# A two-layer decoder on one core: the two norms around the last feed-forward move from VectorE to ScalarE, its first products and its transposes move in TensorE's order, and the output leaves tile by tile

## The chip, the cores and the metric

The kernel runs on one core of a Trainium2 chip. A core has five engines, each with an instruction queue of its own: TensorE (PE, matrix products into PSUM), VectorE (DVE), ScalarE (ACT), GpSimd (POOL) and SyncE (SP, which issues most transfers here). They meet only at semaphores. The metric is the device time in microseconds (us) of one launch.

## The reference

Two decoder layers on x (2 x 512 x 512, 1024 token rows). Each layer is self-attention, cross-attention and a feed-forward, and a layer norm without weights follows each addition:

```python
x = _layernorm(x + _L1_attn_ref(x, ...), axis=-1)
x = _layernorm(x + _L1_xattn_ref(x, ctx_1024, mask, ...), axis=-1)
x = _layernorm(x + _L1_ffn_ref(x, w_gate, w_up, w_down, up_idx, down_idx), axis=-1)
```

The last feed-forward quantises each row of its input to fp8 with the row's own scale, multiplies by the quantised gate and up weights (1408 columns each), takes `silu(g) * u`, quantises that row in the same way and multiplies by the down weights:

```python
qx = _fp8(xr / scale_x)                 # scale_x: largest magnitude of the row / 448
y = qx * scale_x @ (qw * w_scale).T * scale
t = jax.nn.silu(g) * u                  # then quantised and multiplied by w_down
```

`_layernorm` is `(x - m) / sqrt(v + 1e-5)` over the 512 columns of a row.

## The kernel before

The 1024 rows are eight tiles of 128 rows (`NT = 8`), kept in `xf`. Six stages run one after the other, `self0, cross0, ffn0, self1, cross1, ffn1`, and every engine has its own hand-written program for all of them, so the order on an engine is the order of the code. Only the end of `cross1` and the whole of `ffn1` matter here.

**The output projection of `cross1`** (PE, `project`) adds 16 heads into one PSUM bank per tile (bank t for tile t), three bfloat16 matmuls of 128x512 per head and tile. Heads 0 to 7 are done first for all tiles. Then, in before.py, heads 8 to 11 of tiles 0 to 3 go together, and a loop over t finishes each tile: 12 matmuls (4 heads) for tiles 0 to 3, 24 matmuls (8 heads) for tiles 4 to 7. The last matmul of a tile adds one to `y_mm`.

**What follows a tile** in `cross1`: DVE adds the residual and takes mean and variance (`residual`, lines 1028 to 1030, `ln_var`); POOL makes the inverse deviation in two instructions (`inv_std`, lines 612 and 613, `ln_rstd`); DVE normalises (`normalise`, line 1036, `ln_x`); DVE takes the row's largest magnitude and three small scale values (`scales`, lines 994 to 997, `x_amax`); ACT writes two scaled copies (`scaled_x`, lines 734 and 735, `x_scaled`); DVE rounds to fp8 steps in three instructions (`round_x`, lines 1001, 1008, 1011, `qx_ok`); PE transposes the result (`turn_qx`, line 1289, `qx_mm`) and ACT copies it from PSUM (`turned_x`, line 740, `qx_T`). `turn_qx` of tile t < 4 writes bank t, of a later tile bank 6 or 7. DVE runs a loop over k: `residual(k)`, `normalise(k - 1)`, `scales` of k - 1, `round_x(k - 2)`. In PE's loop `turn_qx` of tile t - 4 stands behind the projection of tile t (t = 4 to 7).

**The last feed-forward** (`ffn1`): PE's `product(part, t)` (line 1343) makes gate (part 0, banks 0 to 2) and up (part 1, banks 3 to 5) of a tile, twelve matmuls each. DVE scales them out of PSUM (`gate`, line 1077, and `up`, line 1083), ACT applies silu (line 792), DVE multiplies (`rows`, line 1089) and takes the row's scale values, ACT scales (`scaled_rows`, lines 799 and 800), DVE rounds (`round_t`, lines 1001, 1098, 1102), PE transposes (line 1355), ACT copies (`turned_rows`), PE multiplies by the down weights (line 1374), and DVE adds the residual and takes the statistics (`residual`, lines 1022, 1026, 1029, 1030), POOL the inverse deviation, DVE the norm (line 1036). The loop on DVE per tile:

```python
rows(t)
if t + 1 < NT:
    gate(t + 1)
    up(t + 1)
round_t(t)
if t:
    residual(t - 1)
if t > 1:
    normalise(t - 2)
```

At the end SP waits for all eight norms and stores the whole output with one transfer (line 524).

Of the kernel before, what the change touches and what calls it, by code (L numbers as in the profile page):

```python
# [124 lines left out]
def build(nc, a, out, kept):  # L125
    ctx = ExitStack()
    with ctx:
# [18 lines left out]
        mv = sb("mv", [P, NT, 2], F32)  # L146
        rstd = sb("rstd", [P, NT], F32)
        half_neg = sb("half_neg", [P, QT], F32)
# [228 lines left out]
        def _(sp):  # L377
# [23 lines left out]
            for li, L in enumerate(stages):  # L401
# [111 lines left out]
                if L.masked:  # L513
# [8 lines left out]
                    sp.dma_start(mem[names.index("ffn1")]["sB"][:, :], kept["s"].partition_broadcast(P)).then_inc(s_in, 16)  # L522
            sp.wait_ge(ln_x, NT * len(stages))
            sp.dma_start(out.rearrange("b (p e) d -> p b e d", e=4), xf[:, :, :]).then_inc(out_ok, 16)
            sp.wait_ge(out_ok, 16)


        @block.gpsimd
        def _(pool):
# [75 lines left out]
            for li, L in enumerate(stages):  # L605
                c, m = ledger[li], mem[li]

                def inv_std(k):

                    t = tiles(names[li])[k][0]  # L610
                    pool.wait_ge(ln_var, c["ln"] + k + 1)
                    own(nc.gpsimd.tensor_scalar(rstd[:, t:t + 1], mv[:, t, 1:2], EPS, None, ALU.add))
                    nc.gpsimd.tensor_tensor(rstd[:, t:t + 1], rstd[:, t:t + 1], half_neg[:, 0:1], ALU.pow).then_inc(ln_rstd, 1)

# [107 lines left out]
        def _(act):  # L722
            def x_part(li, n, t, bank):

                act.wait_ge(x_mm, n + 1)
                nc.scalar.activation(xT[0][:, :, token_cols(li, t)], ps[:, bank, :].rearrange("p (c n) -> p c n", c=XC), ACT.Copy).then_inc(x_hi, 1)

            def scaled_x(m, t):

                n = X_COL + t  # L730
                act.wait_ge(x_amax, t + 1)
                if t >= 2:
                    act.wait_ge(qx_ok, t - 1)
                nc.scalar.activation(m["xM"][:, t % 2, :], xf[:, t, :], ACT.Copy, scale=q_up[:, n:n + 1])
                nc.scalar.activation(m["xrow"][:, t % 2, :], xf[:, t, :], ACT.Copy, scale=q_inv[:, n:n + 1]).then_inc(x_scaled, 1)
# [18 lines left out]
            for li, L in enumerate(stages):  # L754
# [34 lines left out]
                if names[li] == "ffn1":  # L789
# [18 lines left out]
                    nc.scalar.preload_act_table_set("silu_and_others")  # L808
                    for t in range(4, 6):
                        turned_x(m, t)  # L810
                    gate(0)
                    for t in range(6, NT):
                        turned_x(m, t)
                    for t in range(NT):
                        scaled_rows(t)
                        if t + 1 < NT:
                            gate(t + 1)
                        turned_rows(t)
                    continue

# [102 lines left out]
                if stages[li + 1] is None and names[li + 1] == "ffn1":  # L923
                    for t in range(NT):
                        scaled_x(mem[li + 1], t)
                        if t >= 4:
                            turned_x(mem[li + 1], t - 4)
                else:
                    for t in range(NT):
                        x_part(li + 1, NT * (li + 1) + t, t, t)  # L930
                        if L.rms and t == 1:
                            f = mem[li + 1]
                            act.wait_ge(q_ok, 15)
                            act.wait_ge(o_mm, c["u"] + UNITS)
                            act.wait_ge(q_kept[0], kept_count(15))
                            act.wait_ge(gu_in[0], 16)
                            nc.scalar.activation(f["gu"][0][:, 0, :, :], f["raw_gu"][0], ACT.Copy).then_inc(gu_hi, 1)
# [3 lines left out]
        def _(dve):  # L941
# [49 lines left out]
            def scales(n, src):  # L991
# [4 lines left out]
                own(nc.vector.reciprocal(q_inv[:, col], q_scale[:, col]))  # L996
                return nc.vector.tensor_scalar(q_up[:, col], q_inv[:, col], 2.0 ** 20, None, ALU.mult)

            def steps(M):
# [13 lines left out]
            for li, L in enumerate(stages):  # L1013
# [58 lines left out]
                if names[li] == "ffn1":  # L1072
# [21 lines left out]
                    def round_t(t):  # L1094
# [7 lines left out]
                        nc.vector.scalar_tensor_tensor(out=q, in0=M, scalar=HALF_UP, in1=y, op0=ALU.max, op1=ALU.subtract, reverse1=True).then_inc(qt_ok, 1)  # L1102

                    dve.wait_ge(s_in, 16)
                    gate(0)
                    up(0)
                    for t in range(NT):
                        rows(t)
# [4 lines left out]
                        if t:  # L1113
                            residual(t - 1)
                        if t > 1:
                            normalise(t - 2)
                    residual(NT - 1)
                    normalise(NT - 2)
                    normalise(NT - 1)
                    continue  # L1120
# [125 lines left out]

                last_attention = names[li + 1] == "ffn1"
                for k in range(NT + 3):
                    if k < NT:
                        residual(k)  # L1250
                    if 0 <= k - 1 < NT:
                        normalise(k - 1)
                        if last_attention:
                            dve.wait_ge(ln_x, c["ln"] + k)
                            scales(X_COL + k - 1, xf[:, k - 1, :]).then_inc(x_amax, 1)
                    if 0 <= k - 2 < NT and last_attention:
                        round_x(mem[li + 1], k - 2)
                    if 0 <= k - 3 < NT and not last_attention:
                        x_part(li + 1, NT * (li + 1) + k - 3, k - 3, k - 3)
# [9 lines left out]
        def _(pe):  # L1269
# [11 lines left out]
            def turn_qx(done, m, t):  # L1281
# [6 lines left out]
                for ch in range(XC):  # L1288
                    last = nc.tensor.transpose(ps[:, bank, :].bitcast(BF16)[:, ch * P:ch * P + P], m["xQ"][:, t % 2, ch * P:ch * P + P], idb[:, :])
                last.then_inc(qx_mm, 1)  # L1290

            pe.wait_ge(const_ok, 4)
# [3 lines left out]
            for li, L in enumerate(stages):  # L1296
# [37 lines left out]
                if names[li] == "ffn1":  # L1334
                    def product(part, t):

                        pe.wait_ge(qx_T, max(t + 1, 3 + part))
                        pe.wait_ge(ln_var, c["ln"] - 2)
                        if t:
                            pe.wait_ge(u_ok if part else g_ok, t)  # L1340
                        for n, (lo, hi) in enumerate(CH):
# [15 lines left out]

                    pe.wait_ge(wt_in, 16 * (2 * XC + IT))
                    product(0, 0)
                    product(1, 0)  # L1360
                    turn_qx(c["ln"], m, 4)
                    turn_qx(c["ln"], m, 5)
# [105 lines left out]
                for h in range(8):  # L1468
                    for t in (4, 5):
                        project(t, h, h == 0, False)  # L1470
                for h in range(8, 12):
                    pe.wait_ge(w_split, c["split"] + H + h + 1)
                    for t in range(4):
                        project(t, h, False, False)
                pe.wait_ge(w_split, c["split"] + 2 * H)
                turns = {4: (0, 1), 5: (2, 3), 6: (4,), 7: (5,), 8: (6,), 9: (7,)}
                for t in range(NT + 2):
                    if t < NT:
                        for h in range(12 if t < 4 else 8, H):
                            last = project(t, h, False, h == H - 1)  # L1480
                        last.then_inc(y_mm, 1)
                    if names[li + 1] == "ffn1":
                        if 4 <= t < NT:
                            pe.wait_ge(idb_ok, 1)
                            turn_qx(c["ln"] + t - 3, mem[li + 1], t - 4)
                    else:
# [63 lines left out]
```

## Time and profile before

| | us |
|---|---|
| median of three runs | 2621.8 (2616.11 to 2622.53) |
| the profiled execution, its time | 2614.38 |
| the profiled execution, its span | 2612.6 |
| PE busy | 2438.2 (93%) |
| DVE busy | 1848.3 (71%) |
| ACT busy | 1588.8 (61%) |
| POOL busy | 711.8 (27%) |

The busy shares are means over six unlike stages. The change touches only what runs after about 2425 us, some 190 us, so the table by stretches of time and the timelines of the engines in that part are what to read, not the shares. A time in a row is counted from the start of the span. The profiled execution took 7.4 us less than the median of the three runs.

### The profile page before, as it was taken

How to read it: one execution, taken by the hardware profiler on the slowest of the kernel's cores; microseconds unless marked ns; L12 is line 12 of the kernel's file. 1: busy time of each engine (PE TensorE's matmuls, PEld its weight loads, DVE VectorE, ACT ScalarE, POOL GpSimd, SP SyncE). 2: the span in 40 equal slices, each digit the busy share in tenths (PEclk: the TensorE clock that was granted, in tenths of full speed). 3: DMA queues.
4: the chain of work that ended last, by engine and by line, in shares of the span. 5: the costliest groups of instructions: out<-in, count | busy, mean ns of one | idle time of the engine just before them, and what ended most of it. 6: DMA issues, size and time to landing. Idle time of an engine off the chain costs nothing. (4 is left out here: it accounts for less than half of the span.)

```text
span 2612.6 us, 57672 instructions
## 1 busy us (share of the span) xinstructions
PE 2438.2 (93%) x21584; PEld 1567.4 (60%) x21584; DVE 1848.3 (71%) x3371; ACT 1588.8 (61%) x2718; POOL 711.8 (27%) x671
## 2 busy tenths in 40 slices
PE   7999998989999999999988999999899999999864
PEld 4555555546666666666465666665566666665432
DVE  4777777657777777776665666667578888884597
ACT  5777675158887777886244566553277777773242
POOL 5666665601111111012332222226100000013111
PEclk9999999999999999999988999999999999999987
DMA  2433335325666666667341444445188777777200
GB/s 93 90 76 87 79 82 127 103 55 108 114 118 110 113 109 117 115 108 154 113 169 26 94 93 96 95 93 139 30 146 149 145 147 144 146 149 153 69 1 32
DMA packets 769429, 273.83 MB, mean 105 GB/s; under 512 B 737905, under 2 KB 740721, under 8 KB 767601
## 3 DMA queue, kind: packets, MB, share of 16 engines
q1 hardware_dynamic: 767504, 265.82, 49.0%
q0 software_dynamic: 1760, 5.77, 0.8%
q8 instruction: 110, 1.80, 0.3%
q14 instruction: 55, 0.44, 0.1%
HBM read 84.55 MB, written 6.44 MB: 35 GB/s over the span
## 5 line engine op out<-in xcount | busy, mean ns | idle before, releaser
L881 ACT ACTIVATE phl<-p,ri 128x1024 bf16<-128x1024 f32 (+4 forms) x512 | 437.4, 854 | 414.0 <-DVE ri L1196 386.1
L1206 DVE SCALAR_TENSOR_TENSOR phl<-p,ri,phl 128x1024 bf16<-128x1024 f32 (+4 forms) x512 | 514.1, 1004 | 103.3 <-issue 75.3
L892 ACT ACTIVATE p<-p,nb 128x1024 f32<-128x1024 f32 (+4 forms) x512 | 435.9, 851 | 53.9 <-DVE nb L1189 39.6
L1273 PE MATMUL ps<-wo_lo,v_hi 128*128 128x128 bf16 x2496 | 440.0, 220 | 0.0
L1272 PE MATMUL ps<-wo_hi,v_hi 128*128 128x128 bf16 x2240 | 396.5, 220 | 23.0 <-DMA wo_hi<-phl 15.7
L1274 PE MATMUL ps<-wo_hi,v_lo 128*128 128x128 bf16 x2240 | 396.2, 220 | 0.0
L1272 PE MATMUL ps<-k_hi,q_hi 128*128 128x512 bf16 (+3 forms) x768 | 272.5, 355 | 20.9 <-DVE nb L1187 18.7
L1273 PE MATMUL ps<-k_lo,q_hi 128*128 128x512 bf16 (+3 forms) x768 | 271.9, 354 | 0.0
L1274 PE MATMUL ps<-k_hi,q_lo 128*128 128x512 bf16 (+3 forms) x768 | 271.7, 354 | 0.0
L1273 PEld LDWEIGHTS ps<-wo_lo,v_hi 128*128 128x128 bf16 x2496 | 245.1, 98 | 33.4 <-issue 0.5
L1272 PEld LDWEIGHTS ps<-wo_hi,v_hi 128*128 128x128 bf16 x2240 | 219.5, 98 | 68.0 <-DMA wo_hi<-phl 27.9
L551 POOL TENSOR_SCALAR wkv_hi<-raw_kv 128x1024 bf16<-128x1024 f32 (+1 forms) x56 | 49.2, 878 | 658.9 <-PE ps L1274 509.5
L1274 PEld LDWEIGHTS ps<-wo_hi,v_lo 128*128 128x128 bf16 x2240 | 219.7, 98 | 0.0
L1272 PE MATMUL ps<-xT_hi,wq_hi 128*128 128x512 bf16 x512 | 195.1, 381 | 4.5 <-DVE xT_lo L958 3.5
L1191 DVE CUSTOM_DVE_ANT_0 p<-ps,rk,nq 128x1024 f32<-128x1024 f32 x128 | 163.1, 1274 | 51.3 <-PE ps L1274 51.0
L1273 PE MATMUL ps<-xT_lo,wq_hi 128*128 128x512 bf16 x512 | 195.1, 381 | 0.0
L1274 PE MATMUL ps<-xT_hi,wq_lo 128*128 128x512 bf16 x512 | 195.1, 381 | 0.0
L1272 PE MATMUL ps<-wo_hi,oT_hi 128*128 128x512 bf16 x512 | 194.4, 380 | 0.6 <-DVE nb L1187 0.6
L1273 PE MATMUL ps<-wo_lo,oT_hi 128*128 128x512 bf16 x512 | 194.2, 379 | 0.0
L1274 PE MATMUL ps<-wo_hi,oT_lo 128*128 128x512 bf16 x512 | 194.1, 379 | 0.0
L651 POOL TENSOR_TENSOR nq<-nq,half_neg 128x4 f32<-128x4 f32 x32 | 32.3, 1010 | 549.6 <-DVE nq L1140 549.6
L1189 DVE CUSTOM_DVE_ANT_0 p<-ps,mb 128x1024 f32<-128x1024 f32 x128 | 155.8, 1217 | 36.5 <-PE ps L1274 34.2
(200 smaller groups left out, 6126.5 us busy)
## 6 DMA issues: line engine op xcount, KB each, us to landing
raw_kv<-in_wkvself SPq DMA_DIRECT2D x32, 512.0 KB, 4.0
raw_q<-in_wqself SPq DMA_DIRECT2D x32, 256.0 KB, 2.6
raw_q<-in_woself SPq DMA_DIRECT2D x32, 256.0 KB, 2.8
raw_q<-in_wqcross SPq DMA_DIRECT2D x32, 256.0 KB, 3.0
raw_q<-in_wocross SPq DMA_DIRECT2D x32, 256.0 KB, 3.0
wo_hi<-phl SPq DMA_TRANSPOSE x384, 3.2
wo_lo<-phl SPq DMA_TRANSPOSE x384, 3.1
raw_kv<-in_wkvcross SPq DMA_DIRECT2D x24, 256.0 KB, 3.2
```

The costliest lines, as they stand in the source:

```text
L551: nc.gpsimd.tensor_scalar(hi, src, 1.0, 1.0, ALU.mult, ALU.mult).then_inc(w_hi, 1)
L651: nc.gpsimd.tensor_tensor(r, r, half_neg[:, 0:QT], ALU.pow).then_inc(q_norm, 1)
L881: nc.scalar.activation(m["ph"](qt, w), m["p"][:, qt % 2, 0:w], ACT.Copy, scale=ri[:, qt % 2:qt % 2 + 1]).then_inc(p_norm, 1)
L892: nc.scalar.activation(prob, prob, ACT.Exp, scale=1.0 if L.rms else -1.0, bias=nb[:, qt % 2:qt % 2 + 1], accum_out=rs[:, qt % 2:qt % 2 + 1 ...
L1189: ins = nc.vector.tensor_tensor_reduce(in1=m["mb"][:, L.batch(n), :], scale=-ISQ, op0=ALU.add, **kw)
L1191: ins = nc.vector.tensor_tensor_reduce(in1=m["rk"][:, n % 2, :], scale=m["nq"][:, n % 2, qt:qt + 1], op0=ALU.mult, **kw)
L1206: nc.vector.scalar_tensor_tensor(out=m["pl"](qt, w), in0=m["p"][:, qt % 2, 0:w], scalar=ri[:, qt % 2:qt % 2 + 1], in1=m["ph"](qt, w), op0= ...
L1272: nc.tensor.matmul(o, l(0), r(0), start=first, stop=False)
L1273: nc.tensor.matmul(o, l(0), r(1), start=False, stop=False)
L1274: return nc.tensor.matmul(o, l(1), r(0), start=False, stop=last)
```

## The change

- **Norms on ScalarE.** In `cross1` and `ffn1` (both stand beside `"ffn1"` in the list of stages) POOL's `inv_std` gets a third instruction, `shift = -mean * rstd`, and ACT normalises with `Identity(x * rstd + shift)`. DVE's `normalise` is gone there. In ACT's program the norm of tile t stands ahead of `scaled_x(t - 1)` in `cross1`, and in `ffn1` the norm of tile t - 1 behind `turned_rows(t)`.
- **Projections tile by tile.** In `cross1` (`L.masked`) heads 8 to 15 of tiles 0 to 3 are done tile by tile as well, so each tile is one run of 24 matmuls.
- **Transposes.** `turn_qx` of tile t - 2 stands behind the projection of tile t (t = 2 to 5), where it was tile t - 4 (t = 4 to 7).
- **First products.** Gate and up of tile 0 move into the projection loop, behind the projections of tiles 6 and 7.
- **DVE's order.** In `cross1` the loop ends with `residual(7)`, `scales` of 6, `round_x(5)`; the rest (`scales` of 7, `round_x(6)`, `round_x(7)`) stands around the first `gate` and `up`.
- **Output.** Eight stores of one tile each, every one behind its tile's norm.

```diff
@@ SP
-            sp.wait_ge(ln_x, NT * len(stages))
-            sp.dma_start(out.rearrange("b (p e) d -> p b e d", e=4), xf[:, :, :]).then_inc(out_ok, 16)
-            sp.wait_ge(out_ok, 16)
+            for t in range(NT):
+                sp.wait_ge(ln_x, NT * (len(stages) - 1) + t + 1)
+                sp.dma_start(out.rearrange("b (p e) d -> p b e d", e=4)[:, t // 4, t % 4, :], xf[:, t, :]).then_inc(out_ok, 16)
+            sp.wait_ge(out_ok, 16 * NT)
@@ POOL, inv_std
+                    own(root)
+                    nc.gpsimd.tensor_scalar(shift[:, t:t + 1], mv[:, t, 0:1], rstd[:, t:t + 1], -1.0, ALU.mult, ALU.mult).then_inc(ln_rstd, 1)
@@ ACT
+            def normalise(li, t):
+
+                act.wait_ge(ln_rstd, ledger[li]["ln"] + t + 1)
+                nc.scalar.activation(xf[:, t, :], xf[:, t, :], ACT.Identity, scale=rstd[:, t:t + 1], bias=shift[:, t:t + 1]).then_inc(ln_x, 1)
...
                     for t in range(NT):
-                        scaled_x(mem[li + 1], t)
-                        if t >= 4:
-                            turned_x(mem[li + 1], t - 4)
+                        normalise(li, t)
+                        if t:
+                            scaled_x(mem[li + 1], t - 1)
+                        if 3 <= t < 7:
+                            turned_x(mem[li + 1], t - 3)
...
-                    for t in range(4, 6):
-                        turned_x(m, t)
+                    turned_x(m, 4)
+                    scaled_x(m, NT - 1)
                     gate(0)
-                    for t in range(6, NT):
+                    for t in range(5, NT):
                         turned_x(m, t)
                     for t in range(NT):
                         scaled_rows(t)
                         if t + 1 < NT:
                             gate(t + 1)
                         turned_rows(t)
+                        if t:
+                            normalise(li, t - 1)
+                    normalise(li, NT - 1)
@@ DVE, ffn1
+                    scaled(NT - 1)
                     dve.wait_ge(s_in, 16)
                     gate(0)
+                    round_x(m, NT - 2)
                     up(0)
+                    round_x(m, NT - 1)
...
                         if t:
                             residual(t - 1)
-                        if t > 1:
-                            normalise(t - 2)
                     residual(NT - 1)
-                    normalise(NT - 2)
-                    normalise(NT - 1)
@@ DVE, end of cross1
+                if names[li + 1] == "ffn1":
+                    for k in range(NT):
+                        residual(k)
+                        if k >= 1:
+                            scaled(k - 1)
+                        if k >= 2:
+                            round_x(mem[li + 1], k - 2)
+                    continue
@@ PE, end of cross1
-                for h in range(8, 12):
+                ahead = 0 if L.masked else 4
+                for h in range(8, 8 + ahead):
...
                     if names[li + 1] == "ffn1":
-                        if 4 <= t < NT:
+                        if 2 <= t < 6:
                             pe.wait_ge(idb_ok, 1)
-                            turn_qx(c["ln"] + t - 3, mem[li + 1], t - 4)
+                            turn_qx(c["ln"] + t - 1, mem[li + 1], t - 2)
+                        if t == 6:
+                            first_product(mem[li + 1], 0)
+                        if t == 7:
+                            pe.wait_ge(ln_var, c["ln"] + 6)
+                            first_product(mem[li + 1], 1)
```

**DVE, one round of its loop at the end of `cross1`.** `xf<-ps,xf` is the residual, `xf<-xf,mv,rstd` the norm, `q_max<-xf` the start of the scales, `xQ<-xM,xrow` the end of the rounding. Before:

```order
L1028 TENSOR_TENSOR xf<-ps,xf 128x512 [waits y_mm]
L1029 BN_STATS stat<-xf 128x6 [waits dve_seq]
L1030 BN_AGGR mv<-stat 128x2 [waits dve_seq]
L1036 TENSOR_SCALAR xf<-xf,mv,rstd 128x512 [waits ln_var,ln_rstd]
L994 TENSOR_REDUCE q_max<-xf 128x1 [waits ln_x]
L995 TENSOR_SCALAR q_scale<-q_max 128x1 [waits dve_seq]
L996 RECIPROCAL q_inv<-q_scale 128x1 [waits dve_seq]
L997 TENSOR_SCALAR q_up<-q_inv 128x1 [waits dve_seq]
L1001 TENSOR_SCALAR xM<-xM 128x512 [waits x_scaled]
L1008 SCALAR_TENSOR_TENSOR xrow<-xM,xrow 128x512 [waits dve_seq]
L1011 SCALAR_TENSOR_TENSOR xQ<-xM,xrow 128x512 [waits dve_seq]
```

Now:

```order
L1049 TENSOR_TENSOR xf<-ps,xf 128x512 [waits y_mm]
L1050 BN_STATS stat<-xf 128x6 [waits dve_seq]
L1051 BN_AGGR mv<-stat 128x2 [waits dve_seq]
L1010 TENSOR_REDUCE q_max<-xf 128x1 [waits ln_x]
L1011 TENSOR_SCALAR q_scale<-q_max 128x1 [waits dve_seq]
L1012 RECIPROCAL q_inv<-q_scale 128x1 [waits dve_seq]
L1013 TENSOR_SCALAR q_up<-q_inv 128x1 [waits dve_seq]
L1022 TENSOR_SCALAR xM<-xM 128x512 [waits x_scaled]
L1029 SCALAR_TENSOR_TENSOR xrow<-xM,xrow 128x512 [waits dve_seq]
L1032 SCALAR_TENSOR_TENSOR xQ<-xM,xrow 128x512 [waits dve_seq]
```

The norm is gone and the rest keeps its order: the rounding of tile k - 2 still stands behind the residual of tile k.

**PE, from the last wait for split weights to the first transpose of `xQ`** (`wo` by `oT` is the projection). Before; 119 further projection matmuls stand at the first "...", which end with tile 4:

```order
L1272 MATMUL ps<-wo_hi,oT_hi 128x512 [waits w_split]
...
L1273 MATMUL ps<-wo_lo,oT_hi 128x512
L1274 MATMUL ps<-wo_hi,oT_lo 128x512
L1289 MATMUL ps<-idb,xQ 128x128 [waits ln_var,qx_ok,idb_ok]
L1289 MATMUL ps<-idb,xQ 128x128 x3
```

Now; the run from that row to the transposes is 72 matmuls and ends with tile 2:

```order
L1294 MATMUL ps<-wo_hi,oT_hi 128x512 [waits w_split]
...
L1295 MATMUL ps<-wo_lo,oT_hi 128x512
L1296 MATMUL ps<-wo_hi,oT_lo 128x512
L1311 MATMUL ps<-idb,xQ 128x128 [waits ln_var,qx_ok,idb_ok]
L1311 MATMUL ps<-idb,xQ 128x128 x3
```

The first transposes, which wait for `qx_ok` of tile 0, moved from behind tile 4 to behind tile 2.

**PE, the first products of `ffn1`** (`qxT` is the transposed input). Before, behind the last projection and a transpose:

```order
L1289 MATMUL ps<-idb,xQ 128x128 x3
L1343 MATMUL ps<-xT_hi,qxT 128x512 [waits ln_var,qx_T,wt_in]
...
L1343 MATMUL ps<-xT_lo,qxT 128x384 x2
L1343 MATMUL ps<-cT_hi,qxT 128x512 [waits ln_var,qx_T]
```

Now, gate of tile 0 between the projections of tiles 6 and 7:

```order
L1296 MATMUL ps<-wo_hi,oT_lo 128x512
L1320 MATMUL ps<-xT_hi,qxT 128x512 [waits wt_in,qx_T]
...
L1320 MATMUL ps<-xT_lo,qxT 128x384 x2
L1294 MATMUL ps<-wo_hi,oT_hi 128x512
```

Gate and up of tile 0 were neighbours; now 24 projection matmuls stand between them.

## Rows read from the trace of the kernel before

**Rows 1.** Busy time by stretch: busy us (x instructions) per engine, granted clock (PEclk), DMA.

```profile
2430.00:2467.00 37.00, 37.00 (x184) 17.17 (x182) 26.78 (x62) 7.15 (x11) 6.77 (x14) 1.00 0.21 68
```

**Rows 2.** Timeline of PE, cross1's projections: start, duration, line, what, count.

```profile
2439.89 0.38 PE L1274 MATMUL ps<-wo_hi,oT_lo 128*128 128x512 bf16 x1
...
2450.47 0.39 PE L1289 MATMUL ps<-idb,xQ 128*128 128x128 bf16 x4
...
2455.87 0.39 PE L1289 MATMUL ps<-idb,xQ 128*128 128x128 bf16 x4
```

**Rows 3.** Timeline of DVE at the end of cross1, same columns, [idle before <-releaser].

```profile
2440.31 0.69 DVE L1028 TENSOR_TENSOR xf<-ps,xf 128x512 f32<-128x512 f32 x1 [0.95 <-PE ps L1274]
...
2448.68 0.68 DVE L1028 TENSOR_TENSOR xf<-ps,xf 128x512 f32<-128x512 f32 x1
...
2450.22 0.53 DVE L1036 TENSOR_SCALAR xf<-xf,mv,rstd 128x512 f32<-128x512 f32 x1
2450.79 0.69 DVE L994 TENSOR_REDUCE q_max<-xf 128x1 f32<-128x512 f32 x1
...
2451.97 0.42 DVE L1001 TENSOR_SCALAR xM<-xM 128x512 int32<-128x512 int32 x1
...
2453.14 0.69 DVE L1011 SCALAR_TENSOR_TENSOR xQ<-xM,xrow 128x512 bf16<-128x512 f32 x1
2453.75 0.68 DVE L1028 TENSOR_TENSOR xf<-ps,xf 128x512 f32<-128x512 f32 x1
```

**Rows 4.** Timeline of PE: the first products of ffn1, gate and then up.

```profile
2474.29 1.01 PE L1343 MATMUL ps<-xT_hi,qxT 128*128 128x512 bf16 x2 [7.22 <-issue]
...
2478.53 0.59 PE L1343 MATMUL ps<-cT_hi,qxT 128*128 128x512 bf16 x2
...
2480.91 0.61 PE L1289 MATMUL ps<-idb,xQ 128*128 128x128 bf16 x8
```

**Rows 5.** Busy time by stretch, columns as in Rows 1: PE just behind pauses.

```profile
2474.30:2478.40 4.10, 4.10 (x12) 1.54 (x13) 2.47 (x7) 2.47 (x4) 0.00 (x0) 0.53 0.00 0
2485.50:2488.60 3.10, 3.04 (x8) 1.15 (x9) 2.98 (x2) 1.42 (x1) 0.00 (x0) 0.54 0.00 0
2595.00:2601.50 6.50, 5.00 (x17) 1.80 (x14) 1.17 (x3) 1.41 (x2) 1.00 (x2) 0.54 0.00 0
```

**Rows 6.** Timeline of DVE in ffn1.

```profile
2483.80 1.61 DVE L1077 TENSOR_TENSOR SG<-ps,sB 128x1408 f32<-128x1408 f32 x1
...
2487.06 1.68 DVE L1089 SCALAR_TENSOR_TENSOR row<-row,q_scale,SG 128x1408 f32<-128x1408 f32 x1
...
2495.93 0.89 DVE L1001 TENSOR_SCALAR M<-M 128x1408 int32<-128x1408 int32 x1 [1.89 <-ACT row L800]
...
2500.06 1.68 DVE L1089 SCALAR_TENSOR_TENSOR row<-row,q_scale,SG 128x1408 f32<-128x1408 f32 x1
...
2513.41 1.68 DVE L1089 SCALAR_TENSOR_TENSOR row<-row,q_scale,SG 128x1408 f32<-128x1408 f32 x1
...
2527.21 1.68 DVE L1089 SCALAR_TENSOR_TENSOR row<-row,q_scale,SG 128x1408 f32<-128x1408 f32 x1
```

**Rows 7.** Timeline of POOL and ACT: small and half-size instructions.

```profile
2513.58 1.58 POOL L612 TENSOR_SCALAR rstd<-mv 128x1 f32<-128x1 f32 x1 [41.82 <-DVE mv L1030]
2515.25 0.57 POOL L613 TENSOR_TENSOR rstd<-rstd,half_neg 128x1 f32<-128x1 f32 x1
2443.72 0.72 ACT L734 ACTIVATE xM<-xf,q_up 128x512 f32<-128x512 f32 x1 [49.34 <-DVE q_up L997]
2517.35 1.47 ACT L799 ACTIVATE M<-row,q_up 128x1408 f32<-128x1408 f32 x1 [3.16 <-DVE q_up L997]
```

**Rows 8.** DMA issues: what, queue, count, KB each, median us from issue to landing.

```profile
out<-xf SPq DMA_DIRECT2D x1, 2048.0 KB, 6.4
kept_gu<-wr SPq DMA_DIRECT2D x22, 128.0 KB, 1.7
kept_d<-gu_hi SPq DMA_DIRECT2D x4, 352.0 KB, 2.5
```

More of the change, by code:

```diff
@@ L146, in build @@
         mv = sb("mv", [P, NT, 2], F32)
-        rstd = sb("rstd", [P, NT], F32)
+        rstd, shift = sb("rstd", [P, NT], F32), sb("shift", [P, NT], F32)
         half_neg = sb("half_neg", [P, QT], F32)
@@ L612, in inv_std @@
                     own(nc.gpsimd.tensor_scalar(rstd[:, t:t + 1], mv[:, t, 1:2], EPS, None, ALU.add))
-                    nc.gpsimd.tensor_tensor(rstd[:, t:t + 1], rstd[:, t:t + 1], half_neg[:, 0:1], ALU.pow).then_inc(ln_rstd, 1)
+                    root = nc.gpsimd.tensor_tensor(rstd[:, t:t + 1], rstd[:, t:t + 1], half_neg[:, 0:1], ALU.pow)
+                    if "ffn1" not in names[li:li + 2]:
+                        root.then_inc(ln_rstd, 1)
+                        return
+                    own(root)
+                    nc.gpsimd.tensor_scalar(shift[:, t:t + 1], mv[:, t, 0:1], rstd[:, t:t + 1], -1.0, ALU.mult, ALU.mult).then_inc(ln_rstd, 1)
                 if L is not None and L.rms:
@@ L997, in scales, with scaled @@
                 return nc.vector.tensor_scalar(q_up[:, col], q_inv[:, col], 2.0 ** 20, None, ALU.mult)
+            def scaled(t):
+                dve.wait_ge(ln_x, ledger[names.index("cross1")]["ln"] + t + 1)
+                scales(X_COL + t, xf[:, t, :]).then_inc(x_amax, 1)
             def steps(M):
@@ L1245, in _ @@
                 quantise_run(LATER.get(L.name, ()))
-                last_attention = names[li + 1] == "ffn1"
+                if names[li + 1] == "ffn1":
[6 more added lines that the diff above has]
+                    continue
                 for k in range(NT + 3):
@@ L1252, in _ @@
                         normalise(k - 1)
[L1253 to L1258, printed above, removed]
+                    if 0 <= k - 3 < NT:
                         x_part(li + 1, NT * (li + 1) + k - 3, k - 3, k - 3)
@@ L1290, in turn_qx, with first_product @@
                 last.then_inc(qx_mm, 1)
+            def first_product(m, part):
+                pe.wait_ge(qx_T, 3 + part)
+                pe.wait_ge(wt_in, 16 * (2 * XC + IT))
+                for n, (lo, hi) in enumerate(CH):
+                    for ch in range(XC):
+                        last = nc.tensor.matmul(ps[:, 3 * part + n, 0:hi - lo], m["qxT"][:, 0, ch, :], m["wT"][part * XC + ch][:, lo:hi], start=ch == 0, stop=ch == XC - 1)
+                last.then_inc(fu_mm if part else fg_mm, 1)
             pe.wait_ge(const_ok, 4)
@@ L1335, in product @@
                     def product(part, t):
[L1337 to L1340, printed above, removed]
+                        pe.wait_ge(qx_T, t + 1)
+                        pe.wait_ge(u_ok if part else g_ok, t)
                         for n, (lo, hi) in enumerate(CH):
@@ L1356, in turn_rows @@
                         last.then_inc(qt_mm, 1)
[L1358 to L1361, printed above, removed]
+                    turn_qx(c["ln"] - 1, m, 4)
                     turn_qx(c["ln"], m, 5)
@@ L1478, in _ @@
                     if t < NT:
-                        for h in range(12 if t < 4 else 8, H):
+                        for h in range(8 + ahead if t < 4 else 8, H):
                             last = project(t, h, False, h == H - 1)
```

## The prediction

> **What bounds the kernel now.** I read the stretches of time first, then PE's, DVE's, POOL's and ACT's timelines behind 2430 us, then the transfers. While the projections of `cross1` run, PE is busy without a pause at the full clock (37.00 of 37 us, clock 1.00) and DVE has room (26.78) [rows 1]. A projection with its transposes comes every 2455.87 - 2450.47 = 5.40 us [rows 2], and DVE's round for a tile takes 2453.75 - 2448.68 = 5.07 [rows 3]. In this stretch the round of DVE started late, so DVE is still at work when PE has finished, and PE waits 7.22 us ahead of the first products [rows 4]. From there on DVE sets the pace: its rounds in `ffn1` follow each other without idle time, 13.35 us apart for the second tile and 2527.21 - 2513.41 = 13.80 from the third [rows 6]. So only what DVE's first `rows` waits for, what lies in DVE's rounds, and the tail can move the end. I follow the start of DVE's first line-1089 instruction, 2487.06 [rows 6], as the mark.
>
> **Projections tile by tile.** The same matmuls in another order. Before, the second tile's residual started at 2440.31 behind 48 + 12 + 12 matmuls [rows 3]; now 72 matmuls are three tiles, so at 2440.31 it is the third tile's (k = 2). Heads 8 to 15 must be split by POOL by then; PE waited for nothing there [rows 1], and the wait for the last head stood ahead of the same first finishing run only 48 matmuls (10 us) later. I take no cost.
>
> **The moved transposes: the step that decides.** PE's transposes of tile t - 2 now stand behind the projection of tile t and wait for `qx_ok` of tile t - 2. DVE gives that at the end of its round k = t, and that round begins with the residual of tile t, that is, when PE has finished the projection in front of the transposes. So PE has to wait for DVE's whole round, and the next projection is queued behind the wait. Before, the transposes were of tile t - 4, whose rounding was two rounds old. From t = 2 to t = 5 PE and DVE therefore take turns. One turn is the sum of:
> - DVE from the residual's start to the end of `xQ`: 2453.14 + 0.69 - 2448.68 = 5.15, less the norm's 2450.79 - 2450.22 = 0.57, so 4.58 [rows 3];
> - four transposes and 24 matmuls, 5.40 [rows 2];
> - the handovers. The last matmul started at 2439.89 and DVE at 2440.31 [rows 2, 3], 0.42, of which 0.22 is that matmul's own slot; so 0.20, and an estimated 0.05 back to PE.
>
> That is 10.23 us at the full clock. **The clock**: behind the pause of 7.22 us and the one of 4 us (from 2480.91 + 0.61 to 2485.5) PE's granted clock, 2.4 GHz before, was at its lower level of 1.2 GHz for a while: 0.53 over 4.10 us and 0.54 over 3.10 [rows 4, 5], which loses 0.47 x 4.10 = 1.9 and 0.46 x 3.10 = 1.4 us. Each turn holds a pause of about 4.8 us, between the two, so I take 1.65, and bounds of 0 and, if PE stays at half speed for the whole projection, 5.1 (the last stretch, 0.54 throughout [rows 5]). A turn is 11.9 us. Four turns: the seventh tile's residual starts at 2440.31 + 4 x 11.9 = 2487.9.
>
> **First products.** Gate of tile 0 goes between two projections, 2480.91 - 2478.53 = 2.38 us at the full clock [rows 4], and then the last projection, 5.18. Its inputs (three turned tiles, weights) are long there. The eighth tile's residual starts at 2487.9 + 7.56 = 2495.5. Up of tile 0 follows beside DVE's work. The 7.22 us wait of PE and the slow start of gate vanish, but the end of the projections has moved from 2467 to 2495.
>
> **DVE up to the mark.** A residual is 2450.22 - 2448.68 = 1.54, the scales 2451.97 - 2450.79 = 1.18, a rounding 2453.75 - 2451.97 = 1.78 [rows 3], scaling gate or up out of PSUM 1.54 (1.61 less the 0.07 by which neighbours overlap) [rows 6]. Behind 2495.5 stand one residual, two scales, three roundings and both scalings: 1.54 + 2.36 + 5.34 + 3.08 = 12.3. Beside it, POOL needs three instructions and ACT the norm: about 2.7 us behind the end of the statistics, while DVE has 2.9 us of other work; no wait. The mark is at 2507.8 instead of 2487.06: **+20.8**.
>
> **First round of `ffn1`.** Before, DVE idled 1.89 us because ACT still had transposes to copy [rows 6]. Now there is time for these between gate and up: **-1.9**.
>
> **Norms off DVE.** In the loop each norm costs 13.80 - 13.35 = 0.45 [rows 6]. Five of them stand ahead of the last `rows`: **-2.25**. The sixth is hidden behind PE's last product. The price of the new POOL instruction is not in the trace; the nearest are 0.57 and, while DVE's line 1089 runs, 1.58 [rows 7]. The first two instructions end at 2515.82; one of 0.45 to 0.57 ends at about 2516.4, ACT's pass of 0.72 at 2517.1, and ACT's next work starts at 2517.35 [rows 7]. So it is hidden, by 0.2 us. By the Trainium skill, GPSIMD Engine Reference, section 1 Specifications, GpSimd shares its SBUF interfaces with VectorE and contends with DVE instructions that have two SBUF inputs; line 1089 has two, and by that rule as by the row only the first of the three instructions is held up.
>
> **The tail.** From the last `rows` to the last statistics nothing changes. Then the third POOL instruction is added (0.5) and ACT's pass of 0.72 stands for DVE's 0.53 [rows 3, 7]: **+0.7**. The last store has 256 KB instead of 2048: between 1.7 (128 KB) and 2.5 (352 KB), by straight line 2.2, against 6.4 [rows 8]: **-4.2** (bounds -4.7 and -3.9). The other seven stores are out long before. The Trainium skill, DMA: Bandwidth & Descriptors, section Anatomy of one DMA, has 2.0 us plus bytes at 436 GB/s, an estimate of 2.6 us for this store and 6.8 for the old one, against which the trace shows 6.4; by the page the sum would be 0.4 us higher.
>
> **Sum.** +20.8 - 1.9 - 2.25 + 0.7 - 4.2 = +13.1 us. Against the profiled execution's own 2614.38 that is 2627.5; against the median of the runs, 2621.8, it is 2634.9. I give 2635, 0.5% slower. A measurement of this kernel tells about 0.3%, 7.9 us, from no change.
>
> **Rivals.**
> - *The clock stays full* in the turns. For it: the pauses are short against 7.22 us. Against it: the pause of 4 us already cost 1.4 [rows 5]. Four times 1.65 less: +6.5, 2628, within 0.3%.
> - *PE never comes back to the full clock* in the turns, since it works half of the time only; the last stretch stayed at 0.54 [rows 5]. Four times 5.1 - 1.65 = 3.45 more: +26.9, 2649. Against it: projections are continuous runs of over 5 us, and a continuous run came back after 4.1.
> - *Faster: the transposes don't wait.* If `qx_ok` of tile t - 2 were there when PE reaches the transposes behind tile t, a turn would be 5.40 instead of 11.9, 26 us less: -12.9, 2609. This is what the edit looks like on PE alone, and DVE could keep up (4.50 per round without the norm). It decides at a turn of 11.9 - 13.1 / 4 = 8.6 us: below it the kernel is faster. Against it is only the order on DVE: the rounding of t - 2 stands behind the residual of t. I may misread a count, no more.
> - *ACT's norms come late in the loop.* If the new POOL instruction took 1.58 us as the held one did, DVE would wait about 0.8 us in each of six rounds: +18, 2640.
>
> **Chances.** The forecast 0.66, full clock 0.10, half clock throughout 0.07, no wait 0.07, late norms 0.10. The bounds of the small terms (store 0.8, handovers 0.5) and 4 us for the medians give the forecast's own range, 2628 to 2641; full clock and late norms are taken in, so 2622 to 2643. Slower by over 0.3%: 0.66 + 0.07 + 0.10 less 0.05 for a forecast that comes out small: 0.78. Faster: 0.08, with 0.01 for an unlisted cause. Within 0.3%: 0.14.
>
> **What would show it.** Right: in the new trace PE idles four times, some 4.8 us each, ahead of the transposes of `xQ` and released by DVE's `xQ`; residuals of tiles 3 to 7 about 11.9 us apart for four of them; granted clock near 0.5 at the start of these projections; the mark near 2508; rounds of 13.35 us in `ffn1` with no idle time; the last store landing in 2 to 2.6 us. Wrong: residuals 5.4 us apart; a clock of 1.00 there; idle time of DVE in the rounds, released by ACT.

## The result and the profile after

| | before | changed |
|---|---|---|
| median, us | 2621.8 (2616.11 to 2624.97) | 2630.4 (2630.07 to 2637.8) |
| ratio | 1 | 1.0048, 95% interval 1.0034 to 1.0061 |
| time of the profiled execution, us | 2614.38 | 2630.4 |
| its span, us | 2612.6 | 2628.6 |
| PE busy | 93% | 92% |
| DVE busy | 71% | 70% |
| ACT busy | 61% | 61% |
| POOL busy | 27% | 27% |

The change makes the kernel 0.5% slower. 0.0048 of 2621.8 us is 12.6 us, between 8.9 and 16.0; the two profiled executions are 16.0 us apart. The overall busy shares hardly move. The cause stands in the timelines behind 2425 us. PE in the changed kernel, where it runs the projections of `cross1` (start, duration, line, what, count, [idle before]):

```profile
2444.79 0.58 PE L1311 MATMUL ps<-idb,xQ 128*128 128x128 bf16 x4 [4.71 <-issue]
2457.83 0.59 PE L1311 MATMUL ps<-idb,xQ 128*128 128x128 bf16 x4 [4.72 <-issue]
2469.47 0.58 PE L1311 MATMUL ps<-idb,xQ 128*128 128x128 bf16 x4 [4.70 <-issue]
2482.12 0.59 PE L1311 MATMUL ps<-idb,xQ 128*128 128x128 bf16 x4 [4.73 <-issue]
```

These are the four moved transposes; PE stands still for 4.7 us ahead of each. The profile puts these waits down to "issue", that is, it names no releaser; that PE waits for `xQ` is read from the times below, and the experiments test it. In [rows 2] the same instructions came 5.40 us apart with no idle time. DVE in the same stretch, the third to eighth residual and one end of a rounding:

```profile
2440.12 0.69 DVE L1049 TENSOR_TENSOR xf<-ps,xf 128x512 f32<-128x512 f32 x1 [2.40 <-PE ps L1296]
...
2444.00 0.69 DVE L1032 SCALAR_TENSOR_TENSOR xQ<-xM,xrow 128x512 bf16<-128x512 f32 x1
2453.15 0.69 DVE L1049 TENSOR_TENSOR xf<-ps,xf 128x512 f32<-128x512 f32 x1 [8.46 <-PE ps L1296]
...
2464.80 0.69 DVE L1049 TENSOR_TENSOR xf<-ps,xf 128x512 f32<-128x512 f32 x1 [7.07 <-PE ps L1296]
...
2477.44 0.69 DVE L1049 TENSOR_TENSOR xf<-ps,xf 128x512 f32<-128x512 f32 x1 [8.07 <-PE ps L1296]
...
2490.59 0.69 DVE L1049 TENSOR_TENSOR xf<-ps,xf 128x512 f32<-128x512 f32 x1 [8.56 <-PE ps L1296]
...
2498.14 0.69 DVE L1049 TENSOR_TENSOR xf<-ps,xf 128x512 f32<-128x512 f32 x1 [2.99 <-PE ps L1296]
```

The third residual is where the second was before, 2440.31 in [rows 3]. `xQ` ends at 2444.00 + 0.69 = 2444.69, and PE's transposes start 0.10 us later, as do the other three behind their own `xQ`. While PE works, DVE idles for 7 to 8.6 us, released by PE; while DVE works, PE idles. The four turns take 13.03, 11.65, 12.64 and 13.15 us, 12.62 on average. The granted clock in the four projections that follow the pauses (stretch, then busy us (x instructions) of PE, PEld, DVE, ACT, POOL, then the clock):

```profile
2445.00:2453.10 8.10, 8.10 (x28) 3.06 (x25) 0.00 (x0) 0.44 (x1) 0.00 (x0) 0.67 0.00 0
2458.00:2464.80 6.80, 6.55 (x27) 2.79 (x26) 0.00 (x0) 0.88 (x2) 0.00 (x0) 0.80 0.00 0
2469.50:2477.40 7.90, 7.90 (x28) 3.14 (x28) 0.00 (x0) 1.10 (x3) 0.00 (x0) 0.70 0.00 0
2482.30:2490.60 8.30, 8.08 (x28) 3.36 (x28) 0.01 (x1) 0.88 (x2) 0.00 (x0) 0.66 0.01 2
```

The first of them, cut where the clock changes:

```profile
2444.79:2450.40 5.61, 5.61 (x17) 2.25 (x18) 0.00 (x0) 0.65 (x2) 0.00 (x0) 0.50 0.00 0
2450.40:2453.10 2.70, 2.70 (x13) 1.02 (x11) 0.00 (x0) 0.00 (x0) 0.00 (x0) 1.00 0.00 0
```

A mean of 0.66 to 0.80 is a mix of the two levels. Each group of transposes and projection starts at 1.2 GHz and comes back to 2.4 GHz in its course, after 5.6, 2.8, 4.8 and 5.8 us, and it lasts up to 8.3 us instead of 5.4. Behind that, `ffn1` on DVE, the starts that answer to [rows 6]:

```profile
2510.47 1.68 DVE L1110 SCALAR_TENSOR_TENSOR row<-row,q_scale,SG 128x1408 f32<-128x1408 f32 x1
...
2521.48 1.68 DVE L1110 SCALAR_TENSOR_TENSOR row<-row,q_scale,SG 128x1408 f32<-128x1408 f32 x1
...
2534.83 1.68 DVE L1110 SCALAR_TENSOR_TENSOR row<-row,q_scale,SG 128x1408 f32<-128x1408 f32 x1
...
2548.18 1.68 DVE L1110 SCALAR_TENSOR_TENSOR row<-row,q_scale,SG 128x1408 f32<-128x1408 f32 x1
```

The mark is at 2510.47 instead of 2487.06, 23.4 us later. From there the changed kernel gains: 11.01 us to the next round against 13.00, and then 13.35 for each of the next six against 13.35 once and 13.80 five times.

### The profile page after: what moved, and what is told of

Its sections match the earlier page's. It is cut to its first block and busy times, and to the rows that moved or that the text cites. A ratio compares the mean times of both kernels' runs of the same rounds, so it can differ in the third digit from the quotient of the medians.

```text
span 2628.6 us, 57440 instructions
## 1 busy us (share of the span) xinstructions
PE 2427.9 (92%) x21345; PEld 1566.0 (60%) x21584; DVE 1837.4 (70%) x3355; ACT 1601.7 (61%) x2734; POOL 716.9 (27%) x687
## 5 line engine op out<-in xcount | busy, mean ns | idle before, releaser
L1295 PE MATMUL ps<-k_lo,q_hi 128*128 128x512 bf16 (+2 forms) x767 | 271.3, 354 | 7.1 <-issue 0.4
L1294 PE MATMUL ps<-k_hi,q_hi 128*128 128x512 bf16 (+3 forms) x640 | 223.2, 349 | 21.9 <-DVE nb L1207 19.8
L1294 PE MATMUL ps<-wkv_hi,xT_hi 128*128 128x128 bf16 x1024 | 174.8, 219 | 1.4 <-DVE rot L1163 1.4
```

Source lines behind the costliest of these rows:

```text
L1294: nc.tensor.matmul(o, l(0), r(0), start=first, stop=False)
L1295: nc.tensor.matmul(o, l(0), r(1), start=False, stop=False)
```

## The experiments

**How they are compared.** The start of this stretch moves by some us from one execution to the next, although the programs ahead of it are the same (the first residual of the kernels with projections tile by tile was at 2424.8 to 2433.1). So beside the ratio of the times, whose interval is 0.1 to 0.2% to each side, the table has the time from the first tile's residual to the end of the span. For kernels with the old order of projections the first residual is taken 36 matmuls x 0.216 (5.18 us for 24 matmuls) = 7.8 us earlier than it was, where tile-by-tile projections would have put it. "Mark" is the start of the first round of `ffn1`, from the same point. Mark and end are read from one profiled execution of each kernel.

| kernel | ratio to before (95%) | mark | to the end |
|---|---|---|---|
| before | 1 | 57.1 | 182.7 |
| changed | 1.0048 (1.0034 to 1.0061) | 80.7 | 198.8 |
| e1_lag3: transposes one tile later | 0.9941 (0.9925 to 0.9957) | 52.2 | 169.4 |
| e2_busy: pauses filled | 1.0019 (1.0007 to 1.0031) | 71.2 | 188.9 |
| e4_swap: DVE rounds ahead of the residual | 0.9961 (0.9948 to 0.9974) | 57.9 | 176.1 |
| e5_turns: before, transposes alone | 1.0115 (1.0094 to 1.0136) | 86.7 | 212.2 |
| e10_two: two of four one tile later | 0.9998 (0.9987 to 1.0009) | 65.6 | 183.1 |
| e6_tiles: before, projections alone | 0.9995 (0.9985 to 1.0005) | 55.3 | 181.0 |
| e7_norms: before, norms of `ffn1` alone | 0.9989 (0.9979 to 1.0000) | 56.8 | 182.2 |
| e3_store: before, stores alone | 0.9993 (0.9981 to 1.0004) | 57.5 | 179.3 |
| e8_late_product: e1, gate behind the last projection | 0.9950 (0.9935 to 0.9965) | 49.5 | 167.3 |
| e9_gate: e1, gate scaled ahead of the last residual | 0.9952 (0.9937 to 0.9967) | 50.7 | 168.8 |

**The place of the transposes (e1_lag3).**

```diff
-                        if 2 <= t < 6:
+                        if 3 <= t < 7:
                             pe.wait_ge(idb_ok, 1)
-                            turn_qx(c["ln"] + t - 1, mem[li + 1], t - 2)
+                            turn_qx(c["ln"] + t - 2, mem[li + 1], t - 3)
```

> The changed kernel with one thing different: the transposes of tile t - 3 stand behind the projection of tile t (t = 3 to 6), so their rounding is one DVE round old. Theory (the turns): no pause of PE, residuals 5.2 to 5.4 us apart, the last one at about 2469.3, the mark (first line that multiplies gate and up) at 2469.3 + 12.3 = 2481.6 instead of 2510.5, span 28.9 us shorter than that of the changed kernel, about 2600, so 12.9 us shorter than the kernel before (0.5% faster). Rival (the long way of the norm over GpSimd and ScalarE is what holds the tiles apart): residuals stay over 10 us apart and the span stays near 2628.

PE's transposes in that kernel:

```profile
2441.93 0.39 PE L1311 MATMUL ps<-idb,xQ 128*128 128x128 bf16 x4
2447.33 0.39 PE L1311 MATMUL ps<-idb,xQ 128*128 128x128 bf16 x4
2452.73 0.39 PE L1311 MATMUL ps<-idb,xQ 128*128 128x128 bf16 x4
2458.14 0.39 PE L1311 MATMUL ps<-idb,xQ 128*128 128x128 bf16 x4
```

No pause, 5.40 us apart. One number in two lines is worth 29.4 us (198.8 - 169.4), 28.9 were expected, and turns the change from 0.5% slower into 0.6% faster than before. Everything else of the change is in this kernel, the long way of the norm over POOL and ACT too, so that rival falls. Of the 13.3 us that it is shorter than the kernel before, 4.9 are won up to the mark, 2.0 in the first round, 2.2 in the next six and 4.1 behind the start of the last.

**The same move in the kernel before (e5_turns).** Only `4 <= t < NT`, tile t - 4 became `2 <= t < 6`, tile t - 2.

> The kernel before with only the transposes moved, those of tile t - 2 behind the projection of tile t (t = 2 to 5); norms, products and output as before. Theory: PE and DVE take turns here too, with the norm on VectorE; turns of about 5.15 + 5.65 plus 2 us for the clock, the last residual at about 2498 instead of 2469, span about 2642, 29 us longer. Rival (ScalarE's norms are needed for the loss): within 8 us of the kernel before.

PE's transposes of tiles 0 and 1 (timeline):

```profile
2451.74 0.58 PE L1289 MATMUL ps<-idb,xQ 128*128 128x128 bf16 x4 [6.00 <-issue]
2462.05 0.59 PE L1289 MATMUL ps<-idb,xQ 128*128 128x128 bf16 x4 [5.30 <-issue]
```

And three residuals behind them on DVE's timeline:

```profile
2456.78 0.69 DVE L1028 TENSOR_TENSOR xf<-ps,xf 128x512 f32<-128x512 f32 x1 [5.14 <-PE ps L1274]
2469.65 0.69 DVE L1028 TENSOR_TENSOR xf<-ps,xf 128x512 f32<-128x512 f32 x1 [7.70 <-PE ps L1274]
2482.90 0.69 DVE L1028 TENSOR_TENSOR xf<-ps,xf 128x512 f32<-128x512 f32 x1 [8.09 <-PE ps L1274]
```

The pauses are longer by the norm, which DVE does here (6.00 and then three of 5.30 against 4.7 us), the turns take 10.3 us for the first and about 13 for the others, and the kernel is 29.5 us longer (212.2 - 182.7). The move alone does it; no other part of the change is needed.

**How many (e10_two).** The transposes of tiles 0 and 1 one tile later, those of tiles 2 and 3 as in the change:

```diff
-                        if 2 <= t < 6:
+                        for k in {3: (0,), 4: (1, 2), 5: (3,)}.get(t, ()):
                             pe.wait_ge(idb_ok, 1)
-                            turn_qx(c["ln"] + t - 1, mem[li + 1], t - 2)
+                            turn_qx(c["ln"] + k + 1, mem[li + 1], k)
```

> The changed kernel with two of the four transposes (tiles 0 and 1) one tile later, two (tiles 2 and 3) where they are. Theory (each transpose that stands behind the projection of its tile plus two costs one turn): two turns of 12.6 us instead of four, 14.5 us less than the changed kernel, 184.3 us from the first residual to the end of the span (198.8 and 169.4 with four and none), so level with the kernel before (182.7). Rival (one such place is enough, the rest follow from it): nearer to one of the two ends.

PE's four transposes:

```profile
2446.48 0.39 PE L1311 MATMUL ps<-idb,xQ 128*128 128x128 bf16 x4
2451.89 0.39 PE L1311 MATMUL ps<-idb,xQ 128*128 128x128 bf16 x4
2456.75 0.58 PE L1311 MATMUL ps<-idb,xQ 128*128 128x128 bf16 x4 [4.48 <-issue]
2469.86 0.58 PE L1311 MATMUL ps<-idb,xQ 128*128 128x128 bf16 x4 [4.72 <-issue]
```

Two places, two pauses, 15.7 us less than with four and 13.7 more than with none, level with the kernel before. The cost is counted by place.

**DVE's order instead of PE's (e4_swap).**

```diff
                     for k in range(NT):
+                        if k >= 2:
+                            round_x(mem[li + 1], k - 2)
                         residual(k)
                         if k >= 1:
                             scaled(k - 1)
-                        if k >= 2:
-                            round_x(mem[li + 1], k - 2)
```

> The changed kernel with PE as it is and DVE's round in another order: the rounding of tile k - 2 ahead of the residual of tile k. Theory (the transposes wait for the whole DVE round because it starts with the residual): now they wait for the rounding alone, which can start when ScalarE's copies are there, 5.0 us behind the residual before; pauses 1.4 to 1.9 us, turns about 7 us, clock mostly full, span 4 x 5.6 = 22 us shorter than the changed kernel's, about 2606. The point from which the change gains was put at turns of 8.6 us, so this should be faster than the kernel before, by about 6 us. Rival (the place on PE matters, not DVE's order): as the changed kernel, 2628.

PE's transposes (timeline):

```profile
2437.04 0.38 PE L1311 MATMUL ps<-idb,xQ 128*128 128x128 bf16 x4 [1.89 <-issue]
2443.89 0.38 PE L1311 MATMUL ps<-idb,xQ 128*128 128x128 bf16 x4 [1.29 <-issue]
```

The start of the first rounding on DVE's timeline:

```profile
2435.06 0.43 DVE L1022 TENSOR_SCALAR xM<-xM 128x512 int32<-128x512 int32 x1 [2.27 <-ACT xrow L746]
```

PE is as in the change, but the transposes wait for the rounding alone, and that waits for ACT's copies. Turns of 6.85 us, pauses of 1.3 to 1.9 us with the clock staying full (1.00 in every stretch from 2425 to 2471), 22.7 us less than the change, and faster than before by 6.6. The loss thus needs both orders together: transposes two tiles behind on PE, and on DVE the residual at the head of the round.

**Wait and clock apart (e2_busy).** Matmuls that nothing uses, in the pauses:

```diff
                             pe.wait_ge(idb_ok, 1)
+                            pe.wait_ge(ln_var, c["ln"] + t - 1)
+                            for _ in range(20):
+                                nc.tensor.matmul(ps[:, t - 2, :], idb[:, :], mem[li]["wo"][0][:, 8, :], start=True, stop=True)
                             turn_qx(c["ln"] + t - 1, mem[li + 1], t - 2)
```

> The changed kernel with 20 matmuls of 128x512 (results unused, into the bank of the transposes that follow) put in each of the four pauses of PE; they start when the residual's statistics are there and take 4.3 us at the full clock, about 1.2 us more than is left of the pause. Theory (wait plus clock): the clock stays at 1.00, each turn is 10.2 us plus 1.2 that the added matmuls outlast DVE's round, 11.4 instead of 12.6, about 5 us less in all; the projection itself 5.2 instead of 8 us. Rival (the clock isn't governed by the pauses): the projections stay at 8 us and the turns get longer, to 13.8, 5 us more in all.

PE's timeline, the added matmuls and the transposes behind them:

```profile
2448.44 4.48 PE L1514 MATMUL ps<-wo_hi,idb 128*128 128x512 bf16 x20
2453.29 0.40 PE L1311 MATMUL ps<-idb,xQ 128*128 128x128 bf16 x4 [0.36 <-DVE xQ L1032]
```

A projection behind such a pause, by stretch (busy us of the engines, then the clock):

```profile
2443.00:2448.40 5.40, 5.37 (x28) 2.59 (x29) 0.00 (x0) 0.72 (x2) 0.00 (x0) 1.00 0.00 0
```

The statistics they wait for are those of tile t - 2, long there, so they started at once and fitted the pause (my 1.2 us for outlasting it was wrong). The profile now names DVE's `xQ` as what the transposes wait for, 0.36 us behind the added work. The clock stays at 1.00 and the four turns are 10.24, 10.26, 10.24 and 10.26 us. So of a turn of 12.62 us, 10.25 is the taking of turns and 2.37 the half clock. Work that nobody needs makes this kernel 10 us faster (198.8 - 188.9).

**The parts that gain, alone.** e6_tiles:

> The kernel before with only the projections tile by tile. Theory: the first residual 7.8 us earlier, but PE then sets the pace with 5.2 to 5.4 us a tile, so the last residual comes 2.1 us earlier than before, and the mark and the end as well; too little for the times. Rival (the head start of DVE is kept): 5 us or more.

By this count the first residual is 7.8 us earlier, the second 5.2, the third 3.3 and the last 2.1 (36.93 us behind the first, 39.03 in the kernel before), the mark 1.8. PE sets the pace: DVE waits a little for PE ahead of its residuals:

```profile
2457.69 0.69 DVE L1028 TENSOR_TENSOR xf<-ps,xf 128x512 f32<-128x512 f32 x1 [0.23 <-PE ps L1274]
2463.10 0.69 DVE L1028 TENSOR_TENSOR xf<-ps,xf 128x512 f32<-128x512 f32 x1 [0.24 <-PE ps L1274]
```

e7_norms:

> The kernel before with only the norms of the last feed-forward on ScalarE (with GpSimd's third instruction). Theory: rounds of 13.35 us instead of 13.80, 5 x 0.45 less up to the last round, 0.45 more at the end, 1.8 us less, which the times can hardly tell; no idle time of DVE in the rounds. Rival (GpSimd and ScalarE come late): DVE waits in each round for ScalarE's scaled rows, rounds of 14 us or more.

Rounds of 13.35 us without idle time, as expected, 2.25 us less over five rounds. But the first round took 14.51 us instead of 13.00: DVE waited 0.89 us for PE's up product, where it didn't wait before, and 2.43 for ACT instead of 1.89. PE's products in that round ran at half clock longer (by stretch, the clock behind POOL's count):

```profile
2484.00:2488.00 4.00, 3.52 (x9) 1.31 (x10) 3.85 (x4) 1.47 (x1) 0.00 (x0) 0.50 0.00 0
2488.00:2492.00 4.00, 4.00 (x17) 1.72 (x15) 3.32 (x5) 0.00 (x0) 0.00 (x0) 0.71 0.00 0
```

In the kernel before, the same products behind the same pause of 4 us were back at the full clock after 2.8 us, here after 5.8; the programs of the two kernels are the same up to there. One execution's clock can hide 1.5 us, and the times don't tell the gain of this part (0.9979 to 1.0000).

e3_store:

> The kernel before with only the output stored tile by tile. Theory: from the issue of the last store to the end of the span 2.8 instead of 6.8 us, 4.0 us (0.15%) less, nothing else. Rival (the seven earlier stores disturb the loop, or the last lands late for a queue of eight): under 2 us.

From the last issue (2603.2) to the end of the span (2606.0) 2.8 us instead of 6.8, a store of 256 KB lands 2.4 us behind its issue. The gain of 4.0 us behind the last issue is in the trace (3.4 in the table, since mark and first round came 0.5 us later); 0.9993 (0.9981 to 1.0004) doesn't tell it from none.

**Where gate belongs (e8_late_product, e9_gate).** Both start from e1_lag3. In e8 `first_product(..., 0)` stands behind the last projection (`t == 7`) instead of in front of it:

> The kernel with transposes one tile later (label e1_lag3), and gate of tile 0 behind the last projection instead of between the last two; up of tile 0 right behind it, as there. Theory (DVE's chain behind the last residual, 12.3 us to the mark, doesn't need gate before 5.7 us of it are over, so gate between the projections only delays the last projection): the last residual 2.4 to 2.75 us earlier than there, the mark and the end as much earlier, 166.7 us from the first residual to the end of the span against 169.4. Rival (gate has to be early, because PE starts late and at half clock otherwise): the mark later by up to 7 us, as PE's wait was in the kernel before.

In e9 DVE's scaling of that gate stands in `cross1`'s loop behind the round k = 6:

> The kernel with transposes one tile later (label e1_lag3), and DVE's scaling of gate of tile 0 ahead of the last residual, where DVE is idle. Theory: 1.54 us leaves the chain behind the last residual, the mark comes 10.8 instead of 12.3 us behind it; 167.9 us from the first residual to the end of the span. Rival: gate isn't ready there and the residual is delayed by more than it saves.

The last residual of e8 on DVE's timeline:

```profile
2469.95 0.69 DVE L1049 TENSOR_TENSOR xf<-ps,xf 128x512 f32<-128x512 f32 x1 [0.83 <-PE ps L1296]
```

The scaled gate and the last residual of e9:

```profile
2469.31 1.62 DVE L1276 TENSOR_TENSOR SG<-ps,sB 128x1408 f32<-128x1408 f32 x1
2472.98 0.69 DVE L1049 TENSOR_TENSOR xf<-ps,xf 128x512 f32<-128x512 f32 x1 [2.05 <-PE ps L1299]
```

e8's residual is 37.16 us behind its first residual, e9's 39.90, like e1's. The mark is 12.33 us behind the last residual in e8 and 10.78 in e9. So gate between the projections costs 2.74 us and gives back 1.55 if DVE uses it there; behind them it is in time anyway. Of the 1.55 us only 0.6 reach the end (169.4 against 168.8). In e1 the last product's residual comes 18.63 us behind the start of the last round and in e9 19.56, with the same code there (e1, then e9):

```profile
2588.58 0.75 DVE L1043 SCALAR_TENSOR_TENSOR yt<-ps,q_scale,sB 128x512 f32<-128x512 f32 x1 [5.28 <-PE ps L1400]
2594.44 0.75 DVE L1043 SCALAR_TENSOR_TENSOR yt<-ps,q_scale,sB 128x512 f32<-128x512 f32 x1 [6.22 <-PE ps L1403]
```

PE's clock came back 5.7 us behind the restart with the last transposes in e1 and 8.2 us in e9. So a difference of under 1 us in the last column can't be put down to an edit. By the traces e8 is the shortest (167.3); the times of e1, e8 and e9 are the same within their intervals, all about 0.5% under the kernel before and 1% under the changed one.

## Why the prediction was right, and where it was off

Forecast 2635 us, +13.1 us; measured +12.6 (8.9 to 16.0) by the ratio, +16.0 by the two spans. The mechanism is the one forecast; one term was too small.

- **Projections tile by tile: right.** The third residual was put at 2440.31 and came at 2440.12. The order of the matmuls was right, and 10.36 us lie between first and third residual; that the two absolute times agree within 0.2 us is luck, since other kernels with this order have it at 2437.0 to 2443.4.
- **The moved transposes: right.** Four pauses of 4.7 us (4.8 forecast). A turn at the full clock was put at 10.23 us, and e2_busy has 10.25.
- **The clock in the turns: the term that was mis-sized.** 1.65 us each were taken from the two nearest rows, [rows 5], and it was 2.37 on average: the slow part behind these pauses lasted 5.6, 2.8, 4.8 and 5.8 us, against 3.8 and 2.8 in the stretches of [rows 5]. Four times 0.7 is 2.9 us, and that is the whole difference between +13.1 and +16.0. The bounds, 0 and 5.1, held it. The rival of a full clock falls by the rows of 0.66 to 0.80, and so does half clock throughout.
- **First products: right in size, and short in judgement.** 7.55 us from the seventh to the eighth residual, 7.56 forecast. The prediction counted the 2.38 us and not that the move brings nothing for it; e8_late_product shows that.
- **DVE up to the mark: right.** 12.33 us, 12.3 forecast. The mark itself was put 20.8 us later (its own terms add up to 20.7) and came 23.6 later by the table, which is the clock term again.
- **First round and norms: right.** 1.99 us gained in the first round (1.9), 2.23 in the next six (2.25). POOL's third instruction took 0.27 us in the loop and ACT's pass 0.81 where 0.45 to 0.57 and 0.72 were assumed, and it is hidden with 0.3 us to spare (POOL's and ACT's timelines of the changed kernel, one round of `ffn1`):

```profile
2590.77 0.27 POOL L619 TENSOR_SCALAR shift<-mv,rstd 128x1 f32<-128x1 f32 x1
2591.07 0.81 ACT L737 ACTIVATE xf<-xf,shift,rstd 128x512 f32<-128x512 f32 x1 [2.04 <-POOL shift L619]
2592.19 1.47 ACT L810 ACTIVATE M<-row,q_up 128x1408 f32<-128x1408 f32 x1 [0.31 <-DVE q_up L1013]
```

  So the rival of late norms falls. The held instruction is again the first one, 1.58 us while line 1110 with its two SBUF inputs runs, as the Trainium skill says of the shared interfaces (GPSIMD Engine Reference, section 1 Specifications).
- **Tail: right within 0.5 us.** From the last product's residual to the last issue 4.64 instead of 4.19 us (+0.45, forecast +0.7); the last product itself came 0.4 us later behind the last round than before, which was not forecast. The store landed in 2.4 us (2.2 forecast from the rows; the prediction's other estimate, 2.6, is by the Trainium skill, DMA: Bandwidth & Descriptors, section Anatomy of one DMA, whose fit is for transfers that GpSimd issues, while this store is issued by SP), and the end comes 4.0 us less behind the issue (4.2).
- **The faster rival** (2609, -12.9 us) was what the edit would give if the transposes didn't wait. They did; one tile later they don't, and e1_lag3 has -13.3 us from the first residual to the end and -15.5 (-19.7 to -11.3) by the ratio. Its deciding point, a turn of 8.6 us, stands as well: 6.85 us (e4_swap) is faster than before, 10.25 (e2_busy) is slower.

That the sum agreed better with the ratio than with the spans is luck: the stretch that the change doesn't touch differs by some us between executions.

## What to carry to other kernels

When a consumer is moved up in an in-order queue, look at what the producer's queue has in front of the item it waits for. If that head waits for the very instructions before the consumer, two engines that overlapped now take turns, and each turn costs the whole round of the other, here 4.7 us of wait and 2.4 us of clock for a transpose of 0.2 us. One step more of distance (`t - 3` for `t - 2`) gave all of it back (29.4 us), and a change of order on the producer gave most of it (22.7, e4_swap). Work put early into a full engine's queue should be asked for by someone early: gate between the projections delayed everything behind it and nobody was waiting.

## What the runs showed of the hardware

- PE's granted clock fell in each of the pauses of 4.0 to 7.2 us shown here and not in those of 1.3 to 1.9 us in e4_swap's projections. In between, it fell in e1_lag3 in a pause of 2.41 us that stood just behind one of 2.08 us and four transposes (the first matmuls of 128x512 behind it take 1.01 us a pair, 0.59 at the full clock):

```profile
2471.13 0.40 PE L1311 MATMUL ps<-idb,xQ 128*128 128x128 bf16 x4 [2.08 <-DVE xQ L1032]
2473.94 1.01 PE L1372 MATMUL ps<-xT_hi,qxT 128*128 128x512 bf16 x2 [2.41 <-DVE SG L1098]
```

- How long PE stayed at the lower level once it worked again varied from 2.8 to 5.8 us behind pauses of the same length: 2.8 us in the kernel before and 5.8 in e7_norms, both behind 4.0 us (by stretch):

```profile
2485.60:2488.40 2.80, 2.80 (x7) 0.98 (x8) 2.69 (x2) 1.32 (x1) 0.00 (x0) 0.51 0.00 0
2484.50:2490.30 5.80, 5.80 (x15) 2.15 (x16) 5.55 (x7) 1.34 (x1) 0.00 (x0) 0.50 0.00 0
```

  So its price is a range, 1.4 to 2.9 us for each pause in the changed kernel.
- Matmuls whose result nothing uses kept the clock full and were worth 2.4 us for each pause.
- The first residual of kernels in which PE's program is the same up to there started at 2424.8 to 2433.1 us. Effects of 2 to 4 us, as the stores and the norms, can be read from a trace and not from the times, and only stretch by stretch: PE's clock alone moved the first round by 1.5 us and the last product by 0.9.
